# Early-fusion transformer block: weighted values two groups at a time in every second round, a third buffer for exponentials, values kept by image

## What is computed

```
h = concat(patches @ W_embed + b_embed + pos, txt)
h = h + attention(layernorm(h))          # 16 heads of 16, causal, softmax in float32
h = h + ffn(layernorm(h))                # RMS-normed ternary 256 -> 1024, gelu, RMS-normed ternary 1024 -> 256
```

## Time and profile before

| | |
|---|---|
| median of three runs | 2130.81 us (2129.62 to 2130.93) |
| the profiled execution | 2129.19 us, its span 2127.5 us |
| mean granted TensorE clock | 0.981 |
| busy in the span: PE | 1987.2 us (93%), 22914 matmuls |
| PE weight loads | 1555.6 us (73%) |
| DVE | 1518.1 us (71%) |
| ACT | 1295.5 us (61%) |
| POOL | 882.0 us (41%) |
| DMA | 93.74 MB, mean 44 GB/s |
| weighted values on PE | 4096 matmuls in 256 groups, 205.2 us busy |
| chain that ended last | PE 85%, DVE 7%, issue 3%, ACT 2% |

### The profile page before, as it was taken

How to read it: one execution, slowest core, us unless ns; L and a number is a source line. 1 busy time by engine, 2 the same in 40 slices (tenths; PEclk the granted TensorE clock), 3 DMA queues, 4 the chain that set the end, 5 groups by cost and what they waited for, 6 DMA issues and landing times.

```text
span 2127.5 us, 58231 instructions
## 1 busy us (share of the span) xinstructions
PE 1987.2 (93%) x22914; PEld 1555.6 (73%) x22914; DVE 1518.1 (71%) x2838; ACT 1295.5 (61%) x2050; POOL 882.0 (41%) x1066
## 2 busy tenths in 40 slices
PE   2789999999999999999999999999999999999875
PEld 2567777777778777777777777877777777777654
DVE  4457778777777677777777767777677787777753
ACT  2346666666666566665666666666566666666552
POOL 0124444444444444443444433444444444444443
PEclk9899999999999999999999999999999999999988
DMA  3111111111111101111101111110111111110000
GB/s 129 25 41 41 48 52 48 32 44 40 52 48 52 47 25 42 49 47 53 48 27 49 41 50 49 50 46 27 43 49 48 52 48 33 43 43 25 28 27 23
DMA packets 62845, 93.74 MB, mean 44 GB/s; under 512 B 9619, under 2 KB 59255, under 8 KB 59497
## 3 DMA queue, kind: packets, MB, share of 16 engines
q1 hardware_dynamic: 62568, 89.90, 15.2%
HBM read 45.03 MB, written 14.94 MB: 28 GB/s over the span
## 4 chain that ended last, share of the span: by engine, by line
PE 85%; DVE 7%; issue 3%; ACT 2%; POOL 1%; DMA 1%; SPq 0%; POOLq 0%; DVEq 0%; ACTq 0%
PE dense L324 45%; PE score L324 25%; PE pvps L324 8%; PE dense L345 3%; PE dense L382 2%; DVE h L1010 1%; PE dense L371 1%; DVE mx L934 1%; POOL acc L1150 1%; DVE km L970 1%; DVE rs L894 1%; DMA borow<-bo 1%; ACT pr L664 1%; DVE st L922 0%; PE dense L533 0%
## 5 line engine op out<-in xcount | busy, mean ns | idle before, releaser
L1131 POOL TENSOR_SCALAR_AFFINE_SELECT pr<-pr 114x456 f32<-114x456 f32 x512 | 303.7, 617 | 939.6 <-ACT pr L664 939.5
L664 ACT ACTIVATE pr<-score 114x1368 f32<-114x1368 f32 x256 | 335.5, 1311 | 337.0 <-PE score L324 336.6
L933 DVE TENSOR_REDUCE mx<-score 114x4 f32<-114x456 f32 x256 | 161.8, 632 | 245.5 <-PE score L324 242.0
L934 DVE TENSOR_REDUCE mx<-score 114x4 f32<-114x912 f32 x256 | 281.3, 1099 | 0.0
L324 PE MATMUL score<-km,qs 32*114 32x114 f32 (+1 forms) x4096 | 222.0, 331 | 24.3 <-issue 16.0
L324 PE MATMUL dense<-wdn,g 128*114 128x256 bf16 x1024 | 239.2, 279 | 4.5 <-issue 4.0
L1150 POOL TENSOR_TENSOR acc<-acc,sq 128x456 f32<-128x456 f32 x192 | 234.0, 1219 | 12.6
L324 PE MATMUL dense<-wdn,gl 128*114 128x256 bf16 x1024 | 234.1, 274 | 0.0
L324 PE MATMUL pvps<-pr,vp 114*32 114x228 f32 (+1 forms) x4096 | 205.2, 318 | 0.5 <-ACT raw L736 0.5
L894 DVE RECIPROCAL rs<-rs 128x228 f32<-128x228 f32 x128 | 201.0, 1570 | 0.0
L324 PE MATMUL score<-qs,km 32*114 32x228 f32 (+1 forms) x4096 | 194.2, 306 | 0.0
(11 more groups left out here) (126 smaller groups left out, 4503.6 us busy)
## 6 DMA issues: line engine op xcount, KB each, us to landing
pix<-x SPq DMA_DIRECT2D x32, 1176.0 KB
rs<-raw SPq DMA_DIRECT2D x256, 57.0 KB, 2.0
cx<-raw SPq DMA_DIRECT2D x256, 57.0 KB, 2.0
out<-h SPq DMA_DIRECT2D x64, 228.0 KB
h<-txt SPq DMA_DIRECT2D x32, 64.0 KB, 7.9
g<-wqkvo SPq DMA_DIRECT2D x1, 1024.0 KB
h<-w_upT SPq DMA_DIRECT2D x1, 1024.0 KB
h<-w_downT SPq DMA_DIRECT2D x1, 1024.0 KB
```

What stands on the lines that cost most here:

```text
L664: act(pr[q % 2][:], score[0:R, :, 0:SW], ACT.Exp, scale=float(HD) ** -0.5).then_inc(a["exp"], 1)
L933: nc.vector.tensor_reduce(mx[:, b, 0, :, r], score[0:R, :, 0:R], AX.X, ALU.max)
L934: nc.vector.tensor_reduce(mx[:, b, 1, :, r], score[0:R, :, R:SW], AX.X, ALU.max).then_inc(v["max"], 1)
L1131: nc.gpsimd.affine_select(out=blocks, in_=blocks, compare_op=ALU.is_ge, fill=0.0, base=0, pattern=[[0, 4], [1, R]], channel_multiplier=-1) ...
```

## The change

- `pr` gets a third buffer. Odd groups always use it (`pr[2]`), even groups take `pr[0]` and `pr[1]` in turn. The exponential of an even group then waits for the weighted values four groups back, that of an odd group for two back, as before.
- On PE, weighted values are done only in odd rounds, two groups in a row: 2 and 3 in R1, 4 and 5 in R3, 6 and 7 in R5, and 0 and 1 of the next pair in R7. Groups 2, 4, 6 and 0 so move from R0, R2, R4 and R6 one round back, past the dense work and row scores between.
- V is made by image rather than by block: the product in R1 gives image 1, that in R4 image 0. `vp` has three slots of two parts: slot 0 for image 0 of every pair, slots 1 and 2 for image 1 by parity. ACT's copy of image 0 waits for group 3 of the pair before, that of image 1 for group 7 of the pair before that.

```diff
--- before.py
+++ after.py
@@ -115,13 +115,13 @@
         selv = sb("selv", [128, Q4], F32)
         tmps = sb("tmps", [128, Q4, 4], F32)
         sel = sb("sel", [128, Q4, R], BF16)
-        vp = sb("vp", [R, 2, 4, H, VW], F32)
+        vp = sb("vp", [R, 3, 2, H, VW], F32)
 
         mx = sb("mx", [R, 2, 2, 4, Q4], F32)
         mr = sb("mr", [R, 2, 2, 4, Q4], F32)
         mp = sb("mp", [R, 2, 2, 4, 32], BF16)
         mT = sb("mT", [128, 2, SW], BF16)
-        pr = [sb(f"pr{i}", [R, 4, SW], F32) for i in range(2)]
+        pr = [sb(f"pr{i}", [R, 4, SW], F32) for i in range(3)]
         rs = sb("rs", [128, 2, S], F32)
         cx = sb("cx", [128, 2, T2], F32)
         raw = sb("raw", [128, 2, 2, S], F32)
@@ -227,6 +227,10 @@
                     return v["max"], count(8, t - back - 1, m // 2 + 1)
                 m -= 1
             return a["w"], 1
+
+        def weights_of(q):
+
+            return pr[2] if q % 2 else pr[(q // 2) % 2]
 
         def bank_of(name, k):
             return dense[:, DENSE.index((name, k)) % 3]
@@ -393,12 +397,13 @@
                                  [q[:, c] for q in aT], c == 0, c == 1)
                 last.then_inc(pe["qk"], 1)
 
-            def values(pair, blk):
-
-                eng.wait_ge(*emptied(pair, "v", blk))
-                for b in range(2):
+            def values(pair, k):
+
+                eng.wait_ge(*emptied(pair, "v", k))
+                b = 1 - k
+                for blk in range(2):
                     for c in range(2):
-                        last = three(bank_of("v", blk)[0:R, b * D:b * D + D],
+                        last = three(bank_of("v", k)[0:R, blk * D:blk * D + D],
                                      [q[:, c, col(blk, b):col(blk, b) + R] for q in aT],
                                      [w[:, 2, c] for w in wa], c == 0, c == 1)
                 last.then_inc(pe["v"], 1)
@@ -515,12 +520,12 @@
                     eng.wait_ge(a["raw"], count(4, pair, gi // 2))
                 elif gi == 0 and began(pair - 1):
                     eng.wait_ge(a["raw"], count(4, pair - 1, 4))
-                P_ = pr[gi % 2]
+                P_ = weights_of(gi)
                 half = r % 2
                 for kb in range(2):
                     for i in range(4):
                         last = mm(pvps[quad(i), half * S + kb * R:half * S + S],
-                                  vp[:, par, 2 * kb + b, 8 * (r // 2) + 2 * i + half],
+                                  vp[:, par + 1 if b else 0, kb, 8 * (r // 2) + 2 * i + half],
                                   P_[:, i, kb * S:S + kb * R], start=(kb == 0), stop=(kb == 1),
                                   skip_group_check=True)
                 last.then_inc(pe["pv"], 1)
@@ -578,9 +583,10 @@
                     if A and k == 7:
                         queries_keys(t, 2)
                         queries_keys(t, 3)
-                    pair, gi = (t - 2, k + 2) if k < 6 else (t - 1, k - 6)
-                    if live(pair):
-                        weighted_values(pair, u if k < 6 else 1 - u, gi)
+                    pair, gi = (t - 2, k + 2) if k < 7 else (t - 1, 1)
+                    if live(pair) and k % 2:
+                        weighted_values(pair, u if k < 7 else 1 - u, gi - 1)
+                        weighted_values(pair, u if k < 7 else 1 - u, gi)
                     if A and k == 0:
                         pixels(t, 0)
                         pixels(t, 1)
@@ -656,12 +662,13 @@
                 if not live(pair):
                     return
 
-                if q >= 2:
-                    eng.wait_ge(pe["pv"], count(8, pair, q - 1))
+                back = 2 if q % 2 else 4
+                if q >= back:
+                    eng.wait_ge(pe["pv"], count(8, pair, q - back + 1))
                 elif began(pair - 1):
-                    eng.wait_ge(pe["pv"], count(8, pair - 1, 7 + q))
+                    eng.wait_ge(pe["pv"], count(8, pair - 1, 8 + q - back + 1))
                 eng.wait_ge(pe["st"], count(8, pair, q + 1))
-                act(pr[q % 2][:], score[0:R, :, 0:SW], ACT.Exp,
+                act(weights_of(q)[:], score[0:R, :, 0:SW], ACT.Exp,
                     scale=float(HD) ** -0.5).then_inc(a["exp"], 1)
 
             def gelu(pair, m):
@@ -693,13 +700,15 @@
                 act(km[:, u, m, 1], bank_of("qk", 2 * m + 1)[:, 0:T2], ACT.Copy,
                     scale=pmask[:, 1:2]).then_inc(a["km"], 1)
 
-            def value_rows(pair, u, blk):
-
-                eng.wait_ge(pe["v"], count(2, pair, blk + 1))
-                if blk == 0 and began(pair - 2):
+            def value_rows(pair, u, k):
+
+                eng.wait_ge(pe["v"], count(2, pair, k + 1))
+                if k == 1 and began(pair - 1):
+                    eng.wait_ge(pe["pv"], count(8, pair - 1, 4))
+                elif k == 0 and began(pair - 2):
                     eng.wait_ge(pe["pv"], count(8, pair - 2, 8))
-                dst = vp[:, u, 2 * blk:2 * blk + 2].rearrange("p b e c -> p (b e) c")[:, :, 0:VW:2]
-                act(dst, bank_of("v", blk)[0:R, 0:2 * D].rearrange("p (e c) -> p e c", c=HD),
+                dst = vp[:, 0 if k else u + 1].rearrange("p x e c -> p (x e) c")[:, :, 0:VW:2]
+                act(dst, bank_of("v", k)[0:R, 0:2 * D].rearrange("p (e c) -> p e c", c=HD),
                     ACT.Copy).then_inc(a["v0"], 1)
 
             def normalized(src, dst, scale, bias, s_out_, s_bias, pair):
@@ -831,7 +840,7 @@
             for i, e in enumerate((-0.5, 0.5)):
                 eng.memset(exps[:, i], e)
             eng.memset(mp[:].rearrange("p b q i c -> p (b q i c)"), 0.0)
-            eng.memset(vp[:].rearrange("p u j e c -> p (u j e c)"), 1.0).then_inc(v["ones"], 1)
+            eng.memset(vp[:].rearrange("p j x e c -> p (j x e c)"), 1.0).then_inc(v["ones"], 1)
             eng.memset(onesf, 1.0).then_inc(v["w"], 1)
             eng.wait_ge(p["w"], 6)
             nc.vector.tensor_reduce(tmpm[:], ident[:].rearrange("p (i y d) -> p y i d", i=4, y=2), AX.X,
@@ -1127,7 +1136,7 @@
                 eng.wait_ge(a["exp"], count(8, pair, gi + 1))
                 apart(eng)
                 for c0 in (0, S):
-                    blocks = pr[gi % 2][:, :, c0:c0 + R]
+                    blocks = weights_of(gi)[:, :, c0:c0 + R]
                     nc.gpsimd.affine_select(out=blocks, in_=blocks, compare_op=ALU.is_ge, fill=0.0, base=0,
                                             pattern=[[0, 4], [1, R]], channel_multiplier=-1).then_inc(p["mask"], 1)
 
```

## The result

The changed kernel takes 2183.26 us (median of 4 runs, 2182.36 to 2184.71) against 2130.87 on the same chips: ratio 1.0246, interval 1.0228 to 1.0264. It is slower by 52 us. The forecast was 2181, in a range of 2158 to 2201.

A forecast was written before the change was run, and what follows sets the result against it. PE's order of work was taken as the bound, with even-round groups merely covering waits for DVE or ACT. +1.76 us a step over 29 steps (+51), -2 and +1 made +50 on 2129.19; with 1.6 for the median, 2181, range 2158 to 2201.

The forecast's parts named there:

- A second group costs 0.59: Odd rounds on PE: a weighted-values group right behind another adds 0.59 us, four times +2.36 a step.
- R0 to R1, -0.00: Up to R1's first V product: removing R0's group gains nothing; row scores' 0.36 us is lost waiting for DVE.
- R2, -0.00 and R4, -0.00: First up product (R2) and first down product (R4): removing the group gains nothing, as PE already waits for DVE.
- the second rival: No-change case: only the exponential's cover counts, not DVE; R0 and R4 lose 0.51 against 0.52 won; 2131, chance 0.05.
- R6, -0.6: R6: removing the group lets DVE's final sums start earlier, giving back 0.6 of its 0.72 us.
- Third buffer and V by image, nothing: The added buffer and reordered V production only allow the late groups and cost or gain nothing themselves.
- The sum: A full step: 2.36 less 0.6 gives +1.76 us, times 29 steps +51.
- The lighter steps, +1: Steps at both ends of the run: 0 to +2.4 us, taken as +1.
- The loop's turns, -2: Five places where the loop starts anew: longer queued PE work may hide idle time, 0 to -3 us, taken as -2.
- that the switches pay: Faster rival: PE time alone counts, 0.13 us won per pair of groups, -15 in all; 2116, chance 0.07.
- That only the exponential counts: No-change rival: waits for the exponential lose 0.51 us in R0 and R4 against 0.52 won; 2131, chance 0.05.
- That one wait is not bound: Milder slower rival: one of three even-round waits has hidden slack, 0.65 us back each step; 2162, chance 0.07.

The follow-up runs named there:

- e3: As e1, but group 4 alone moved from R2 to R3, in front of group 5: 2147.74 us, ratio 1.0083 to the kernel before.
- e4: As e1, but group 0 alone moved from R6 to R7, in front of group 1: 2133.17 us, ratio 1.0010 to the kernel before.
- e2: As e1, but weighted values of groups 2, 4 and 6 left out altogether: 2132.69 us, ratio 1.0013 to the kernel before.
- e5: Changed kernel, first quarter of R4's down products waiting only for the four hidden parts it reads: 2165.17 us, ratio 1.0157 to the kernel before.
- e8: Changed kernel with R2's feed-forward input transposes and copies put ahead of the embed products: 2154.72 us, ratio 1.0117 to the kernel before.
- e1: Changed kernel with every weighted-values group back in its own round, third buffer and V by image kept: 2130.42 us, ratio 1.0004 to the kernel before.
- e10: Changed kernel with the edits of e5 and e8, only groups 4 and 0 moved: 2123.70 us, ratio 0.9962 to the kernel before.
- e7: Groups paired in even rounds instead of odd, three buffers in another turn, accumulator copies and repacking later: 2151.52 us, ratio 1.0088 to the kernel before.
- e6: Kernel before with the looser R4 wait of e5, nothing moved: 2128.20 us, ratio 0.9978 to the kernel before.
- e9: Kernel before with the looser wait of e6 and the turned order of e8, nothing moved: 2133.75 us, ratio 1.0007 to the kernel before.

## Why the prediction was right

Against its own steps:

- **A second group costs 0.59.** 0.58 measured, in four rounds and in e3 and e4.
- **R0 to R1, -0.00.** R0 and R1 together are 0.57 longer: the 0.30 that R0 wins is lost again, as forecast, and the group's own 0.58 is left. (It wins 0.30 and not the 0.36 of the prediction, because the row scores start 0.15 behind the exponential, 1148.42 against 1146.96 + 1.31 = 1148.27, and not 0.06.) The row scores wait for ACT and the V product for DVE; e2 shows the same with the island out altogether.
- **R2, -0.00 and R4, -0.00.** Exact in the changed kernel. That these waits took the place of the islands is shown from both sides: taking the group out wins nothing (e2), and making the wait come earlier sets the time free (e5: 0.49, with the exponential next; e8: 0.79). For R4 the second rival had 0.57 from its rows; in most steps of the kernel before the row scores start 0.55 behind the exponential and not 0.63 as in the step that was read, and 0.55 less the 0.06 of a released wait gives the 0.49.
- **R6, -0.6.** 0.65 measured.
- **Third buffer and V by image, nothing.** e1.
- **The sum.** +1.76 a step was +1.65: 48 us over 29 steps.
- **The lighter steps, +1.** What lies ahead of the 29 full steps and behind them is 1.3 us longer in the profile.
- **The loop's turns, -2.** This term is not borne out. I had thought that a longer queue of PE work might hide part of PE's idle time at a turn. It hides none (2.9 to 3.5 us, against 3.1 to 3.4 before), and the turns take 6 us more in the profile of the changed kernel than in that of the kernel before. Half of that can be chance: e1, with nothing moved, has 3 us more as well (last section).

Between the two profiles the time grew by 54.9 us (2184.11 less 2129.19), of which 48, 6 and 1 are these terms. The forecast of 50 was 3 too high in the steps and 8 too low at the turns, and these errors partly cancel. That the medians then lie only 2 us from it (2183.26 against 2181) owes something to luck: the profiled execution of the kernel before lies 1.7 us under its median, that of the changed kernel 0.9 over its own.

The rivals: that the switches pay needed 0.72 us to spare at the three waits, and there is none; the prize of 0.13 for a pair is real, though, and e10 collects it. That only the exponential counts falls with R2, where there is time to spare for it and nothing came back. (That rival's sum also leaves out the 0.12 that R6 does not give back; with it the rival would stand at 2134 and not at 2131.) That one wait is not bound falls with e2.

The Trainium skill's sentence that matmul busy time is a bad measure of how close a kernel is to its limit (Trainium Kernel Development and Optimization, section Performance Expectations) fits what was seen: 1987 us of it before and after, with 52 us between the two times. The Trainium skill's rule that changing the tiling mode drains the engine (TensorEngine Tiling (Array Packing), section Key Properties) fits as well, by the 0.58 us of a second group against the 0.72 of one that stands alone; taken alone it would have led to the wrong sign.

## What to carry to other kernels

Work on the fullest engine is free where it stands between an event and a wait for another engine's answer to it, as long as it ends before the answer comes; before moving such work, read for each place it leaves how long ahead of the next product its input was ready, and count what it costs only where that time is large. A distance that is the same small number in every step (0.05 to 0.06 or 0.14 to 0.15 us here) is a wait, even where the profile shows the engine as busy. And price the steps at both ends and the turns of a loop too: in e7 18 of 30 us lay outside the full steps. To win from fewer switches, first bring the answer forward (an earlier order, a wait for no more than is read), then move the work.

## What the runs showed of the hardware

At each of the five turns of the loop PE stands still, for 3.1 to 3.4 us in the kernel before and 2.9 to 3.5 in the changed one (the line "score <- issue" has 16.0 and 15.9 us, 5 times). Behind most turns (four of five before, all five in the changed kernel) the granted clock goes to the lower level, 1.2 GHz. Three stretches of 3.4 us at one turn, of the kernel before and then of the changed one:

```profile
1238.00:1241.40 3.40, 2.47 (x25) 2.18 (x26) 0.48 (x1) 0.74 (x1) 0.00 (x0) 0.79 0.27 80
1241.40:1244.80 3.40, 3.40 (x25) 3.25 (x27) 1.84 (x4) 0.00 (x0) 0.00 (x0) 0.71 0.79 183
1244.80:1248.20 3.40, 3.40 (x67) 2.58 (x63) 3.17 (x13) 2.55 (x4) 1.07 (x2) 1.00 0.83 191
```

```profile
1271.00:1274.40 3.40, 2.27 (x21) 1.70 (x22) 0.00 (x0) 0.09 (x1) 0.00 (x0) 0.50 0.50 121
1274.40:1277.80 3.40, 3.40 (x18) 3.40 (x18) 1.65 (x2) 0.00 (x0) 0.00 (x0) 0.51 0.87 222
1277.80:1281.20 3.40, 3.12 (x45) 2.69 (x44) 2.69 (x6) 1.37 (x2) 0.00 (x0) 1.00 0.44 102
```

At this turn the lower level lasts about twice as long in the changed kernel, 6.8 us for 3.4 (the second stretch has 18 matmuls for 25). Over all profiles the time at the lower level goes with what the turns cost. The second column is that time within the 29 full steps; the third is by how much the two steps on either side of each turn are longer than two median steps, summed over the five turns:

| us | at 1.2 GHz | extra of the turns |
|---|---|---|
| e2 | 10 | 21.7 |
| e3 | 10 | 20.9 |
| e5 | 14 | 20.2 |
| e8 | 14 | 21.6 |
| kernel before | 17 | 23.2 |
| e1 | 24 | 26.5 |
| e4 | 24 | 25.3 |
| e6 | 27 | 26.9 |
| e10 | 27 | 26.5 |
| e9 | 31 | 27.8 |
| changed kernel | 34 | 29.2 |

Three more us at the lower level cost about one (an estimate: 29.2 less 20.9 over 34 less 10). e7 falls out of the row, with 18.7 for 24; part of its lower level lies away from the turns. Kernels that differ in nothing near the turn fall on either side (e1 has the order of work on PE of the kernel before, and 3.3 us more), so I can't say that the change causes its 6; what decides how long the lower level lasts was not tried.
